# Token weights plus a number, multiplied into the hidden rows out of PSUM, with a factor folded into w2's rows

## The reference, cut to what matters

```
x = x + L0(gn(x))
z = gn(x)
scores = softmax(z_tokens @ gate_w + gate_b)          # per token, 4 experts
top_v, top_i = top_k(scores, 2);  top_w = softmax(top_v)
present[k, e] = expert e was somebody's k-th choice    # any token: 0 or 1
coef[e] = sum_k present[k, e] * top_w[k]               # one number a token
hdn  = relu(z @ w1[e] + b1[e])                         # 96 hidden rows an expert
y[e] = hdn @ w2[e] + b2[e]
out  = x + sum_e coef[e] * y[e]
```

## Time and profile before

| | |
|---|---|
| time, median of 3 runs | 169.03 us (168.38 to 169.12) |
| the profiled execution | 168.52 us, of which the profile's span is 166.7 us |
| busy PE / DVE / ACT / POOL | 149.2 / 140.5 / 110.8 / 64.6 us |
| granted clock of TensorE | 1.0 (2.4 GHz) over the whole span |

### The profile page before, as it was taken

How to read it: one execution, slowest core, us unless ns; L and a number is a source line. 1 busy time by engine, 2 the same in 40 slices (tenths; PEclk the granted TensorE clock), 3 DMA queues, 4 the chain that set the end, 5 groups by cost and what they waited for, 6 DMA issues and landing times.

```text
span 166.7 us, 3638 instructions
## 1 busy us (share of the span) xinstructions
PE 149.2 (89%) x1291; PEld 118.4 (71%) x1291; DVE 140.5 (84%) x385; ACT 110.8 (66%) x250; POOL 64.6 (39%) x77
## 2 busy tenths in 40 slices
PE   0499899999989999997999999979998979789973
PEld 0499799999989999996999998846653422223321
DVE  2887997769999899899999889766757979999993
ACT  3485298659496493793895638763949699867830
POOL 7040224505237067175167227205125014854530
PEclk9999999999999999999999999999999999999999
DMA  5682123410504105014013000000000000112113
GB/s 139 173 233 63 22 65 96 137 29 4 153 10 128 32 4 150 11 45 118 0 52 116 0 4 0 0 6 0 0 0 0 0 0 4 47 47 88 56 49 94
DMA packets 8698, 9.06 MB, mean 54 GB/s; under 512 B 3624, under 2 KB 7496, under 8 KB 8680
## 3 DMA queue, kind: packets, MB, share of 16 engines
q1 hardware_dynamic: 8536, 8.59, 18.7%
q10 hardware_dynamic: 144, 0.24, 0.5%
HBM read 2.28 MB, written 1.57 MB: 23 GB/s over the span
## 4 chain that ended last, share of the span: by engine, by line
PE 48%; DVE 22%; ACT 13%; issue 5%; POOL 4%; DMA 3%; SPq 1%; DVEq 0%; ACTq 0%
DVE v_acc L1316 6%; PE qk_ps L858 5%; PE qk_ps L860 5%; DVE h_mixed L1597 4%; ACT h_mixed L612 4%; PE mix_ps L976 3%; ACT hidden L584 3%; DMA x_sb<-in_x 2%; PE mix_ps L1142 2%; PE out_ps L953 2%; DVE stats L1270 2%; POOL x_sb L791 2%; PE qk_ps L847 2%; PE qk_ps L849 2%; PE qk_ps L848 2%
## 5 line engine op out<-in xcount | busy, mean ns | idle before, releaser
L1316 DVE SCALAR_TENSOR_TENSOR v_acc<-v_ps,v_taps,v_acc 96x544 f32<-96x544 f32 x60 | 46.6, 777 | 4.8 <-ACT v_acc L480 3.7
L858 PE MATMUL qk_ps<-w_a,x_a 128*128 128x192 f16 x243 | 46.6, 245 | 0.4 <-DMA x_c<-x_lo 0.4
L860 PE MATMUL qk_ps<-w_b,x_b 128*128 128x192 f16 x243 | 46.5, 245 | 0.0
L858 PEld LDWEIGHTS qk_ps<-w_a,x_a 128*128 128x128 f16 x243 | 24.5, 101 | 0.8 <-issue 0.7
L860 PEld LDWEIGHTS qk_ps<-w_b,x_b 128*128 128x128 f16 x243 | 23.6, 97 | 0.3
L1597 DVE TENSOR_TENSOR h_mixed<-h_mixed,hidden 128x512 f32<-128x512 f32 x24 | 21.4, 941 | 1.2 <-ACT h_mixed L612 1.2
L791 POOL TENSOR_TENSOR x_sb<-x_sb,xn 96x512 f32<-96x512 f32 x8 | 14.3, 1788 | 19.6 <-ACT xn L590 19.6
L863 PE MATMUL qk_ps<-w_c,x_c 96*128 96x192 f16 x81 | 20.1, 248 | 0.0
L753 POOL TENSOR_TENSOR sq_sum<-qk_sq 128x384 f32<-128x384 f32 x7 | 7.0, 999 | 29.6 <-ACT qk_sq L497 24.9
L556 ACT ACTIVATE sc_exp<-sc_qk,neg_max 96x12 f32<-96x12 f32 x16 | 4.7, 296 | 16.9 <-DVE neg_max L1361 16.9
L762 POOL TENSOR_TENSOR rstd<-var_eps,minus_half 96x2 f32<-96x2 f32 (+2 forms) x9 | 8.5, 944 | 19.1 <-DVE var_eps L1296 19.1
(11 more groups left out here) (228 smaller groups left out, 384.6 us busy)
## 6 DMA issues: line engine op xcount, KB each, us to landing
x_b<-x_a SPq DMA_DIRECT2D x7, 324.0 KB, 3.1
x_sb<-in_x SPq DMA_DIRECT2D x8, 192.0 KB, 3.9
out<-xs SPq DMA_DIRECT2D x7, 192.0 KB, 2.1
x_a<-x_lo SPq DMA_DIRECT2D x7, 108.0 KB, 2.4
x_b<-x_lo SPq DMA_DIRECT2D x7, 108.0 KB, 2.3
x_c<-x_lo SPq DMA_DIRECT2D x21, 36.0 KB, 1.9
w_sb<-in_L_conv_w SPq DMA_DIRECT2D x2, 144.0 KB
cst<-in_consts ACTq DMA_DIRECT2D x1, 236.0 KB, 3.6
```

The source lines that it names most:

```text
L858: eng.matmul(to, window(x_a[p][:, dx, b], half, dy), w_a[:, t, :], start=(t == 0), stop=False, skip_group_check=True)
L860: mm = eng.matmul(to, window(x_b[p][:, dx, b], half, dy), w_b[:, t, :], start=False, stop=False, skip_group_check=True)
L1316: eng.scalar_tensor_tensor(out=v_acc[i % 3][:, :, :], in0=v_window(dy, dx), scalar=v_taps[:, t:t + 1], in1=v_acc[i % 3][:, :, :], op0=ALU. ...
```

## The change

- `coefs` is gone. `mix(i)` reads w0 from the PSUM bank and does (w0 + `token_add`) * hidden in one SCALAR_TENSOR_TENSOR, for each block. `token_add` is s1 / s0 (s1 * s0, since s0 is 1 or -1). Where s0 is 0, w0 + 2^26 * s1 takes its place and 2^-26 is the factor.
- The factor `row_mult` (s0, or 2^-26 * s1) goes into `w2T`'s rows: `scale_w2`, three ACT instructions of 128x96 after relu(19). Six small DVE instructions make `token_add` and `row_mult` after gate_split(0).
- Waits: `mix(i)` waits for weight(i) itself, `bias_tile(i)` for all of mix(i) (except that in the last pair mix waits for the bias tile), and `weight(i)` for mix(i - 2) and bias_tile(i - 2).
- RELU_DVE shrinks to (6, 7): relus 18, 20 and 22 go to ACT.
- Order: gates 5, 6, 7 follow each other on PE, with first(8) and first(9) behind them; on ACT high_xn2(5) to (7) and gate_exps(1) stand ahead of relu(8). `turn_u(0)` moves from behind first(21) to behind first(19), `weight(0)` from behind first(22) to behind first(21). gate_weights(1) and gate_split(1) stand ahead of mix(1), and top_exps(1) ahead of bias_tile(0).
- The preparation of w1 and w2 moves one iteration later on DVE, PE and ACT (prep_w1 from 4 to 5, prepare/copy/low of w1 from 5 to 6, of w2 from 6 to 7).

```diff
...
 HT = PAIRS * MT
+BIG = 2.0 ** 26
...
 STATS_BEFORE = [1, 3, 5, 7, 10, 12, 13, 15, 16]
-RELU_DVE = (6, 7, 18, 20, 22)
+RELU_DVE = (6, 7)
 ONE_TAP = (2, 3, 4, 5)
...
         slope = sb("slope", [128, 2, MT])
         bias_col = sb("bias_col", [C, 2])
...
         w0_done = sem("w0_done")
         b2_ready = sem("b2_ready")
...
+                eng.wait_ge(w0_done, i + 1)
+                if i < PAIRS - 1:
+                    eng.wait_ge(mixed_done, MT * (i + 1))
                 wait(eng, x1_biased, i - 1)
...
-            def coefs(i):
-                eng.wait_ge(w0_done, i + 1)
-                if i == 0:
-                    eng.wait_ge(slope_ready, 1)
+            def scale_w2():
+                eng.wait_ge(factors_set, 2)
+                eng.wait_ge(w2_set, 1)
                 for m in range(MT):
-                    wait(eng, second_done, MT * (i - 2) + m + 1 if i >= 2 else 0)
-                    eng.activation(h_mixed[i % 2][:, m, :], w0_ps[i % 2], ACT.Identity, scale=slope[:, 0, m:m + 1],
-                                   bias=slope[:, 1, m:m + 1]).then_inc(coef_set, 1)
+                    a = eng.activation(w2T[:, m, :], w2T[:, m, :], ACT.Copy, scale=row_mult[:, m:m + 1])
+                a.then_inc(w2_scaled, 1)
...
                     copy_proj()
-                if i == 5:
+                if i == 6:
                     copy_w1()
-                if i == 6:
+                if i == 7:
                     copy_w2()
...
             normalise2(7)
-            relu(8)
+            high_xn2(5)
+            high_xn2(6)
+            high_xn2(7)
             gate_exps(1)
-            high_xn2(5)
-            relu(9)
-            high_xn2(6)
-            relu(10)
-            high_xn2(7)
-            for h in (11, 12, 13, 14):
+            for h in range(8, 15):
                 relu(h)
             top_exps(0)
-            for h in (15, 16, 17):
+            for h in range(15, 19):
                 relu(h)
             take_u(0)
-            for h in (19, 21):
-                relu(h)
-            coefs(0)
-            relu(23)
+            relu(19)
+            scale_w2()
+            relu(20)
+            relu(21)
             eng.wait_ge(bias_done, 1)
             eng.copy(bias_col[:, :], small_ps[0:C, BIAS:BIAS + 2]).then_inc(bias_ready, 1)
+            relu(22)
+            relu(23)
+            top_exps(1)
             eng.wait_ge(bias_ready, 1)
             bias_tile(0)
-            top_exps(1)
-            coefs(1)
             bias_tile(1)
...
                     take_u(1)
-                coefs(i)
                 bias_tile(i)
...
                 eng.wait_ge(w1_step, 5)
-                eng.wait_ge(mix_ready, 4)
+                eng.wait_ge(mix_ready, 5)
                 for m in range(MT):
...
             def prepare_w2():
-                eng.wait_ge(mix_ready, 5)
+                eng.wait_ge(mix_ready, 6)
                 for m in range(MT):
...
                     eng.wait_ge(proj_set, 1)
-                if a == 4:
+                if a == 5:
                     eng.wait_ge(w1_lo_set, 1)
-                if a == 5:
+                if a == 6:
                     eng.wait_ge(w2_set, 1)
...
                     prepare_proj()
-                if i == 5:
+                if i == 6:
                     prepare_w1()
-                if i == 6:
+                if i == 7:
                     prepare_w2()
...
             gate(5, 0, 8, 24)
-            first(8)
             gate(6, 0, 8, 24)
-            first(9)
             gate(7, 0, 8, 24)
-            for h in range(10, 12):
+            for h in range(8, 12):
                 first(h)
...
                 else:
-                    eng.wait_ge(coef_set, MT * (i - 1))
+                    eng.wait_ge(mixed_done, MT * (i - 1))
                     eng.wait_ge(b2_ready, i - 1)
...
-            for h in range(18, 22):
-                first(h)
+            first(18)
+            first(19)
             turn_u(0)
-            first(22)
+            first(20)
+            first(21)
             weight(0)
...
                .then_inc(bias_done, 1)
+            first(22)
             first(23)
...
                     eng.wait_ge(logit_free, PAIRS)
+                    eng.wait_ge(w2_scaled, 1)
                 elif i == 1:
...
                     x_stats(7)
-                if i == 4:
+                if i == 5:
                     prep_w1()
-                if i == 5:
+                if i == 6:
                     low_w1()
...
             gate_split(0)
-            relu(18)
-            relu(20)
+            eng.wait_ge(slope_ready, 1)
+            eng.tensor_scalar(equal[:, 0, :], slope[:, 0, :], 0.0, BIG, ALU.is_equal, ALU.mult)
+            eng.tensor_scalar(equal[:, 1, :], slope[:, 0, :], 0.0, 1.0 / BIG, ALU.is_equal, ALU.mult).then_inc(equal_set, 1)
+            eng.wait_ge(equal_set, 1)
+            eng.tensor_tensor(moved[:, 0, :], equal[:, 0, :], slope[:, 0, :], ALU.add)
+            eng.tensor_tensor(moved[:, 1, :], equal[:, 1, :], slope[:, 1, :], ALU.mult).then_inc(moved_set, 1)
+            eng.wait_ge(moved_set, 1)
+            eng.tensor_tensor(row_mult[:, :], moved[:, 1, :], slope[:, 0, :], ALU.add).then_inc(factors_set, 1)
+            eng.tensor_tensor(token_add[:, :], moved[:, 0, :], slope[:, 1, :], ALU.mult).then_inc(factors_set, 1)
             gate_scores(1)
-            relu(22)
...
             def mix(i):
+                eng.wait_ge(w0_done, i + 1)
+                if i == 0:
+                    eng.wait_ge(factors_set, 2)
+                if i == PAIRS - 1:
+                    eng.wait_ge(b2_ready, PAIRS)
                 for m in range(MT):
                     wait_hidden_taken(eng, MT * i + m)
-                    eng.wait_ge(coef_set, MT * i + m + 1)
-                    eng.tensor_tensor(h_mixed[i % 2][:, m, :], h_mixed[i % 2][:, m, :], hidden[:, i, m, :], ALU.mult)\
-                       .then_inc(mixed_done, 1)
+                    wait(eng, second_done, MT * (i - 2) + m + 1 if i >= 2 else 0)
+                    eng.scalar_tensor_tensor(out=h_mixed[i % 2][:, m, :], in0=w0_ps[i % 2], scalar=token_add[:, m:m + 1],
+                                             in1=hidden[:, i, m, :], op0=ALU.add, op1=ALU.mult).then_inc(mixed_done, 1)
...
             mix(0)
-            mix(1)
             gate_weights(1)
             gate_split(1)
+            mix(1)
             add(0)
...
```

More of the change, by code:

```diff
@@ L180, in build @@
         slope = sb("slope", [128, 2, MT])
+        equal = sb("equal", [128, 2, MT])
+        moved = sb("moved", [128, 2, MT])
+        token_add = sb("token_add", [128, MT])
+        row_mult = sb("row_mult", [128, MT])
         bias_col = sb("bias_col", [C, 2])
@@ L314, in build @@
         w0_done = sem("w0_done")
-        coef_set = sem("coef_set")
+        equal_set = sem("equal_set")
+        moved_set = sem("moved_set")
+        factors_set = sem("factors_set")
+        w2_scaled = sem("w2_scaled")
         b2_ready = sem("b2_ready")
```

## The result

The changed kernel takes 162.81 us (median of 4 runs, 162.42 to 164.02), beside 169.0 us for the kernel before on the same chip. The ratio is 0.9653, with an interval from 0.9594 to 0.9712. The prediction was 162.5 us. Some executions run about 2 us longer at a granted clock of 0.99; ratios are formed without them, medians over all runs. The profiled execution took 163.14 us, with a span of 161.3 us, and the granted clock was 1.0 (2.4 GHz) throughout, as before.

The account below looks back on a forecast made before the run. DVE, its products held by POOL's adds, was taken to bound the last stage, PE close behind. Gains 3.85 + 1.5 + 1.0 = 6.35 us take 168.52 to 162.2; 162.5 was said, forecast 161.0 to 163.7, range 160.8 to 165.3.

Parts of the forecast that it names:

- the loop: From second(0) to the first half's last product: 27.55 us before, 23.7 after, PE bound, gain 3.85 us.
- four periods: Last stage, pairs after turn_u and the second weight: PE at 3.04 us a pair, 12.16 us in all.
- the one wait: Ahead of second(1), PE waits 0.75 us for mix(1)'s first product; bounds 0 to 1.1 us.
- The hold in gate_split(1): Ahead of mix(1), one of six small DVE instructions is held 1.05 us by POOL's add.
- Part 3: Ahead of the last stage: gates in a row, earlier first(18), second(0) at 133.9 instead of 135.39 despite turn_u(0)'s wait; gain 1.5 us.
- the wait for top_exps(0): On ACT ahead of relu(15): about 1 us, costing nothing as first(19) needs that relu just when it comes.
- Part 4: w1's preparation one iteration later: PE's wait for k_diag in iteration 5 goes; gain 1.0 us, bounds 0 and 1.26.
- The 0.25 given back: copy_w2 stands ahead of ACT's last copy of qk, which waited 0.46 for PE, so 0.25 us is lost.
- The first rival: Last stage: the new products still take the port with POOL, 0.96 us each in the mean; time 166.6 us, chance 0.08.
- The second: Waits at k_diag, turn_u and relu(15) eat the gains outside the loop; only 3.85 us left, 164.7 us, chance 0.15.
- The third: Slower: DVE and POOL lock every time, 1.16 us a product; 170.9 us, decides from about 1.09, chance 0.03.
- the fourth: No hold at gate_split(1) and all of the 1.26 us at k_diag: 161.4 us, within the forecast, no chance of its own.

Follow-up runs that it names:

- four moves: Changed kernel with turn_u(0), relu(8), top_exps(1) and the channel means reordered and POOL's first add held until gate_split(1) is over: 161.8 us beside 162.86.

## Why the prediction was right, point by point

**The bound and the loop.** The prediction read the earlier trace rows as a mutual lock of DVE's products and POOL's adds, and PE as the engine that is late next. Both hold. Expected against measured: a mix 2.0 against 1.98, DVE's period 2.60 against 2.57, PE's 3.04 against 3.07, the loop 23.7 against 23.53. The four periods in the sum took 0.13 us more than 12.16, weight and the one wait 0.92 instead of 1.07, and the last two pairs 4.37 instead of 4.52, so small misses cancelled in part. The hold in gate_split(1) was 0.95 us (1.12 against 0.17) for one of its six instructions, against 1.05 expected; which one it would be wasn't said. The Trainium skill states that GpSimd and a vector instruction with two SBUF inputs keep each other out of a shared port pair (SBUF — State Buffer, SBUF: two separate sides). The changed kernel and the one with w0 in SBUF agree: 753 ns at most from PSUM, up to 1755 ns from SBUF. The Trainium skill also says that VectorE is closer to SBUF and ScalarE to PSUM, to be used accordingly (Advanced Engine Details and Errata, The Read-Write Bubble). A price for the PSUM operand was not seen here: 738 to 740 ns from PSUM, 742 from SBUF, as medians.

**Part 3** was to give 1.5 us and gave 1.25. The parts around its end came as worked out: from first(18) to second(0) 6.1 us expected and 6.09 measured, the six factor instructions 0.77 us against 0.9, mix(0) at 132.23 against 132.5. The step that was off is first(18), 1.18 us earlier by the sum and 0.93 by the trace. DVE, ACT, POOL and PE from the last logits on show why, and last POOL's row of the kernel before:

```profile
121.17 0.21 DVE L1385 SCALAR_TENSOR_TENSOR logits<-mix_ps,gate_b_sb 128x48 f32<-128x48 f32 x1 [0.94 <-PE mix_ps L982]
...
121.67 1.20 DVE L1409 TENSOR_TENSOR g_in<-logits,g_max 128x64 f32<-128x64 f32 x1
123.19 0.77 DVE L1426 TENSOR_TENSOR beaten<-g_exp 128x48 f32<-128x48 f32 x1 [0.32 <-ACT g_exp L607]
...
122.91 0.26 ACT L607 ACTIVATE g_exp<-g_in 128x64 f32<-128x64 f32 x1 [1.42 <-DVE g_in L1409]
...
120.52 3.38 POOL L753 TENSOR_TENSOR xn_lo<-xn,xn_hi 96x512 f16<-96x512 f32 x3 [2.87 <-ACT xn_hi L587]
...
123.79 0.39 PE L998 MATMUL qk_ps<-xn_hi,w_hi 96*128 96x512 f16 x1 [0.17 <-ACT hidden L592]
```

```profile
124.06 3.47 POOL L747 TENSOR_TENSOR xn_lo<-xn,xn_hi 96x512 f16<-96x512 f32 x3 [6.27 <-ACT xn_hi L579]
```

Counted from gate(5), the logits came 1.15 us earlier, not 1.3: the 24 products of the gates in a row take 2.84 us from start to start, where the three sets of before take 2.69. And the three high_xn2, moved ahead, also moved POOL's three low_xn2 ahead, from 124.06 to 120.52, onto DVE's small instructions just behind the logits: g_in took 1.20 us, where it took 0.22 before. (With the gates back, POOL's three rows start at 123.06, behind it, and it takes 0.23.) ACT waited 1.42 us for it, and relu(8) stood behind that wait, so first(12) started 0.33 us later than it would have behind first(11). These two are 0.48 us; the sum had left about 0.2 of room (ten firsts of 0.65 and 0.22 for the present products would give 127.6, and it said 127.8), and the difference is the missing 0.25. The prediction had moved ACT's instructions past each other and not asked what POOL does behind them, though it had the same lock in the last stage. It also counted the wait for top_exps(0) at 1 us (0.24 measured) and that for u_tok at 1.0 (0.74), neither of which changed when second(0) came: from first(18) on the path took what was said.

**Part 4** was to give 1.0 us and gave 0.63, within its bounds of 0 and 1.26. Its first half is right: k_diag takes 0.17 us again and PE waits for it nowhere. The 0.25 given back has the wrong source and is too small. ACT's last copy of qk behind copy_w2 delays nothing (PE's lead over the kernel with the preparation back is 0.63 us on both sides of it). What comes back is the 0.72 us of a wait in iteration 6 that the prediction put at nothing; the wait that went was worth 1.35 us, not 1.26. It placed the 2.3 us of prep_w1 "where DVE is ahead by about that much", with no term for what stands between prep_w1 and the taps: two small instructions, the channel means and take_logits(0). PE waits for the latter right at the head of iteration 6.

```profile
80.62 0.44 DVE L1234 TENSOR_REDUCE max_w<-w_sb 128x3 f32<-128x288 f32 x1
...
81.65 0.79 DVE L1244 TENSOR_SCALAR w_back<-w_row_max 128x3 f32<-128x3 f32 x1
...
83.21 0.13 DVE L1385 SCALAR_TENSOR_TENSOR logits<-small_ps,gate_b_sb 128x16 f32<-128x16 f32 x1
...
83.49 0.30 PE L889 MATMUL small_ps<-mv,cst 96*96 96x4 f32 x2 [0.51 <-DVE logits L1385]
```

**The sum and the rivals.** The sum was 6.35 us. The stages give 5.90, the medians 6.2: the loop gave 0.17 more than its term, parts 3 and 4 together 0.62 less. That the median came within 0.3 us of the number is luck in part, since the start ahead of the first mark alone varies by more. The first rival (DVE stays held) fell with the 753 ns. The second (the first two gains stay away) fell: 1.88 of 2.5 us came. The 0.6 are missing by the kind of thing it named, a wait in iteration 6 and one behind ACT's relus, though not at the places it named (k_diag, turn_u, relu(15)). The third needed 1.09 us a product, the fourth no hold at gate_split(1) and all of 1.26; four moves puts the wait behind that hold at 0.57 us.

## What to carry to other kernels

Before work is taken off an engine because its instructions are long, look whether they are long or only held: one operation with 682 ns in the median and 1757 at most, beside an equally stretched row on another engine, says held. Here, in the last stage's loop, one PSUM operand in the same place was worth 4 us, and taking 18.6 us of work off ACT nothing. A moved instruction carries with it what waits for it on other engines (here POOL's low halves), and ahead of each wait of the next engine all its releasers must be asked, not only the largest. To compare two traces, take stages between marks: apart from one of 0.18 us they repeated to some hundredths of a us, while the spans differed by up to 1.8 us through their first 16 us.

## What the runs showed of the hardware

- The holds strike small instructions too: a cast of 16 columns took 1.12 us instead of 0.17, an instruction of 3 columns in prep_w1 (w_back) 0.79 instead of the 0.14 it takes in four moves, g_in 1.20 instead of 0.22, each beside a POOL row of 0.99 us or more. Of the DVE instructions with a PSUM input, none in the traces of before and after takes 0.1 us more than the shortest of its line and shape.
- It goes the other way as well, for four columns too. In the kernel before with 4-column adds, six of POOL's eight rows were 0.20 us; the two that began while products ran were 0.62 and 1.60 (DVE's three products of 1.89 us begin at 141.22). The longer one ends 0.6 us after these products do, which no run here explains:

```profile
142.11 1.60 POOL L791 TENSOR_TENSOR x_sb<-x_sb,xn 96x4 f32<-96x4 f32 x1 [2.47 <-ACT xn L590]
...
148.05 0.20 POOL L791 TENSOR_TENSOR x_sb<-x_sb,xn 96x4 f32<-96x4 f32 x1 [2.49 <-ACT xn L590]
```

- Which product is held isn't the same each time: with w0 in SBUF the mix at 143.15, three products, took 2.06 us (none held) and the next 3.07. In the two profiles of four moves, one program, prep_w1's w_row_max was held in one (0.86 us) and its w_top in the other (0.99), and with that PE's wait behind them was 0.55 and 0.73 us.
